# Moving the S4 kernel row's chain: vectors before denominators on GpSimd, residue product in tile 4's up place, kernel row's products and sums in three places

## The chip, the cores and the metric

One core of a Trainium2 chip (trn2) runs the kernel. Its engines are TensorE (PE in the profile), VectorE (DVE), ScalarE (ACT), GpSimd (POOL) and SyncE (SP), which here only starts transfers. The metric is the device time of one execution in microseconds.

## The reference

Input is x, 2048 rows of 512 values (2 x 1024 x 512), float32. With xn the layer norm of each row:

```
s   = causal convolution of xn, along its 512 columns, with a kernel row K, + D * xn
g   = silu( W2' ( silu(W1' xn) * (W3' xn) ) )      W' = W + 2 * B A   (LoRA, rank 16)
out = x + s * g
```

W1' and W3' are 1376 x 512, W2' is 512 x 1376. K (512 values) comes from an S4 model of 64 complex states:

```
B = Vc @ Bp ;  denom[l, n] = g[l] - Lambda[n]
k00, k01, k10, k11 = sum_n v[n] / denom[l, n]    for v = Ct*B, Ct*p, q*B, q*p (Ct, q conjugated)
K = real(ifft(c * (k00 - k01 * k10 / (1 + k11))))
```

K does not depend on x, so it is worked out once, while the first block of rows runs.

## The kernel before, in words

**Blocks and tiles.** The 2048 rows are taken as 4 blocks (`NBLK`) of 512. `body` treats one block: the 1376 hidden units are cut into 11 tiles (`HT`, j = 0 to 10) of 128, the last of 96. Each tile has three places, "gate", "up" and "down". In TensorE's program tile j is: `hidden` for W1' ("gate", into bank h1), `hidden` for W3' ("up", into h3), then `down(b, j - 1)`, the W2' product of the tile before, which adds into four banks f0 to f3. Matrices are split into a high and a low part, and `three` (lines 939 to 941) issues three matmuls per product, so `hidden` and `down` are 12 matmuls each. After tile 10 follow the last `down` and the convolution (`convolve`).

**What a tile costs the other engines.** ScalarE: silu of h1 into g (L615) and the high part of g into ghl (`hidden_hi`, L632), which waits for `g_used`, TensorE's signal that the `down` before has read ghl. VectorE: g times h3 (`hidden_mul`, L792) and the low part into ghl (`hidden_lo`, L797). Both parts of ghl are wanted by `down(b, j)`.

**Folds, first block only.** The LoRA product of each weight tile is made by TensorE in one of two spare banks (`fold`, L921 and L926), added to the raw weights by VectorE (`fold_add`, L728), rounded to the high part by ScalarE (`fold_hi`, L592), and the low part is made by VectorE (`fold_lo`, L743 or L740), three of them by GpSimd (`POOL_LO`). `folds(place, j)` says which fold stands where: (1, j+2) in gate, (3, j+2) in up, (2, j) in down. TensorE waits for the low part of (2, j) in `wait_split` ahead of `down(b, j)`, that is in tile j + 1. The two spare banks are taken in turn (`spare_table`), and a fold waits for `spare_free`, which VectorE gives after the `fold_add` of the use before. In the first block VectorE makes the low part of the last fold of a place at the start of the next place (`late`). `rows_moments` (L752, L755) for the next block also stand on VectorE at tiles 4 to 6.

**The chain of the kernel row K, first block only.** It runs beside the tiles, in this order:

1. GpSimd makes -Lambda and 2/step (`small_ready`); ScalarE scales the trigonometric rows (L671, `den_ready`, tile 1 gate).
2. GpSimd adds up the denominators and their squared magnitude (four 128x512 products and sums, `mag_ready`), then makes its three fold lows, then B and the vectors `vmat` (38 instructions on 1 to 64 columns, `v_ready`).
3. VectorE inverts mag in two halves (`RECIPROCAL_AT`, L860).
4. GpSimd multiplies by it (`res_ready`, two instructions).
5. TensorE makes the four sums over the states (L1056, `KAPPA_AT`) in a spare bank; ScalarE copies them out (L675) in its own program at the same place, and the spare bank is free only after that copy.
6. GpSimd does the complex arithmetic on 128x4 pieces, stores the coefficients (`coef_scratch`, L1268) and, when they have landed, loads them back as a row on all partitions (`coef_row`, L1273).
7. VectorE multiplies the four parts of the DFT matrix by that row (L849, `K_PRODUCTS_AT`) and sums each over its 512 columns (L853, `K_SUMS_AT`).
8. GpSimd stores the row, spreads and skews it with two more transfers into `tz`; ScalarE and GpSimd split it (tile 9 up, `tz_hi`, `tz_lo`) for the convolution.

Every engine executes its own list in order, and semaphores are all that ties the lists together. The order is written by hand, by the tables of places at the head of the file. On VectorE, within one place, the order before is: `hidden_mul` (up only), the late fold low, the fold adds, products, sums, `hidden_lo` (up only), reciprocal, moments.

Of the kernel before, what the change touches and what calls it, by code (L numbers as in the profile page):

```python
# [25 lines left out]
ALU = mybir.AluOpType  # L26
# [150 lines left out]
MOMENTS_AT_FIRST = {(4, "down"): (0,), (5, "down"): (1,), (6, "down"): (2, 3)}  # L177
MOMENTS_AT = {(r, "down"): (r,) for r in range(RT)}

RECIPROCAL_AT = [(2, "down"), (3, "down")]  # L180

KAPPA_AT = (5, "gate")
K_PRODUCTS_AT, K_SUMS_AT = (7, "gate"), (7, "up")
TOEPLITZ_AT = (9, "up")


# [60 lines left out]
def build(nc, x, xT, w1, w3, w2, lora, lora_st, lora_mv, s4_lanes, s4_vc, s4_bp, s4_scalars, trig, lanes, dft, outT):  # L247
    ctx = ExitStack()
    with ctx:
# [468 lines left out]
        def _(dve):  # L718
# [108 lines left out]
            def body(b, par, par_next, first, last):  # L827
                norm_at = NORM_AT_FIRST if first else NORM_AT
                split_at = SPLIT_AT_FIRST if first else SPLIT_AT
                moments_at = MOMENTS_AT_FIRST if first else MOMENTS_AT  # L830
                late = []
                for j in range(HT):
                    for place in ("gate", "up", "down"):
                        if place == "up" and not (first and j == 0):
                            hidden_mul(b, j)
                        if first:
                            now = folds(place, j)
                            for f_ in late:
                                fold_lo(*f_)
                            for f_ in now:  # L840
                                fold_add(*f_)
                            for f_ in now[:-1]:
                                fold_lo(*f_)
                            late = now[-1:]
                        if first and (j, place) == K_PRODUCTS_AT:
                            dve.wait_ge(dft_in, 16)
                            dve.wait_ge(coef_row_in, 16)
                            for h in range(K_PARTS):
                                nc.vector.tensor_tensor(dft_sb[:, h, :], dft_sb[:, h, :], coef_row[:, :], ALU.mult) \  # L849
                                    .then_inc(k_products, 1)  # L850
                        if first and (j, place) == K_SUMS_AT:
                            dve.wait_ge(k_products, K_PARTS)
                            nc.vector.tensor_reduce(kcol[:, :], dft_sb[:, :, :], AXIS.X, ALU.add).then_inc(k_summed, 1)  # L853
                        if place == "up":
                            hidden_lo(b, j)
                        if first and (j, place) in RECIPROCAL_AT:
                            n = RECIPROCAL_AT.index((j, place))
                            dve.wait_ge(mag_ready, 1)
                            part = mag[:, n * D // len(RECIPROCAL_AT):(n + 1) * D // len(RECIPROCAL_AT)]
                            nc.vector.reciprocal(part, part).then_inc(inv_ready, 1)  # L860
                        for c in () if last else norm_at.get((j, place), ()):
                            next_shift(b + 1, c, par_next)
                        for c in () if last else split_at.get((j, place), ()):
                            next_lo(b + 1, c, par_next)
                        for r in () if last else moments_at.get((j, place), ()):
                            rows_moments(b + 1, r)
                if not last:
                    for c in norm_at["out"]:
                        next_shift(b + 1, c, par_next)
                    for c in split_at["out"]:  # L870
                        next_lo(b + 1, c, par_next)
                if last:
                    last_sum(b, par)
                else:
                    out_sum(b, par)
# [249 lines left out]
        def _(pool):  # L1125
            steps = [0]

            def then(ins):

                steps[0] += 1  # L1130
                ins.then_inc(s4_step, 1)
                pool.wait_ge(s4_step, steps[0])
# [4 lines left out]
            def tt(out, a, c, op):  # L1137
                return nc.gpsimd.tensor_tensor(out, a, c, op)  # L1138
# [50 lines left out]


            pool.sem_inc(small_ready, 1)
            pool.wait_ge(den_ready, 3)
            then(tt(den_im[:, :], den_im[:, :], res[:, :], ALU.add))
            then(tt(mag[:, :], den_re[:, :], den_re[:, :], ALU.mult))
            then(tt(res[:, :], den_im[:, :], den_im[:, :], ALU.mult))
            tt(mag[:, :], mag[:, :], res[:, :], ALU.add).then_inc(mag_ready, 1)
            for kind, j in POOL_LO:
                fold_lo(kind, j)

            then(ts(vtmp[:, 0:1], lane_d[:, 3:4], lane_c[:, SIGN:SIGN + 1], ALU.mult))  # L1200
            then(ts(vtmp[:, 1:2], lane_d[:, 5:6], lane_c[:, SIGN:SIGN + 1], ALU.mult))
            pool.wait_ge(bvec_in, 32)
# [17 lines left out]

            ts(vmat[:, :], vmat[:, :], lane_c[:, SIGN:SIGN + 1], ALU.mult).then_inc(v_ready, 1)
            pool.wait_ge(v_ready, 1)

            pool.wait_ge(inv_ready, len(RECIPROCAL_AT))
            tt(res[0:NS, :], den_re[0:NS, :], mag[0:NS, :], ALU.mult).then_inc(res_ready, 1)
# [51 lines left out]
            rows_rstd(1, 2)  # L1277


            pool.wait_ge(k_summed, 1)  # L1280
            tt(kcol[0:1, 0:1], kcol[0:1, 0:1], scal[0:1, 0:1], ALU.add).then_inc(k_done, 1)
            pool.wait_ge(k_done, 1)
            pool.dma_start(k_row[0, P:P + D].rearrange("(p h) -> p h", h=K_PARTS), kcol[:, :]).then_inc(k_stored, 16)
# [71 lines left out]
```

## Time and profile before

| | us |
|---|---|
| median of 3 runs | 411.18 (411.14 to 411.35) |
| the profiled execution | 411.04 |
| its span (first to last instruction) | 409.2 |
| TensorE busy | 403.8 |
| VectorE, ScalarE, GpSimd busy | 169.0, 106.6, 70.7 |
| TensorE's granted clock | 1.0 of full speed in all slices |

Times of rows are counted from the start of the span. Between span and device time lie 1.84 us. A matmul's shown length overlaps the next one's; the distance between starts is what it costs. The first block takes about the first 117 us of the span.

### The profile page before, as it was taken

The page shows a single profiled execution, that of the slowest core. Times are in us where ns is not written, and L with a number is a line of the kernel's source. Part 1 is how long each engine was busy: PE and PEld are TensorE (multiplying, and loading weights), DVE is VectorE, ACT ScalarE, POOL GpSimd, SP SyncE. Part 2 cuts the span into 40 slices and gives each one's busy share as a digit, 9 for nine tenths or more (in the row PEclk, how much of TensorE's full clock was granted, in tenths as well). Part 3 has the DMA queues.
Part 4 walks back from the last instruction along what each step waited for, and adds up shares of the span by engine and source line. Part 5 has one row for each costly group of instructions (what it writes and reads, how often), then busy time and mean ns, then how long its engine had stood idle before and what let it go on. Part 6 is the DMA issues. An engine that isn't in the chain of part 4 may idle for free.

```text
span 409.2 us, 5001 instructions
## 1 busy us (share of the span) xinstructions
PE 403.8 (99%) x1850; PEld 336.9 (82%) x1850; DVE 169.0 (41%) x264; ACT 106.6 (26%) x174; POOL 70.7 (17%) x140
## 2 busy tenths in 40 slices
PE   8999999999999999999999999999999999999996
PEld 8988888878888888888888888888888888888885
DVE  5777776783792322142343222133334111211125
ACT  7654332222351111222221111112222111111122
POOL 6237737510800114000000102300000000000000
PEclk9999999999999999999999999999999999999999
DMA  7673933403425101000016101000002000000002
GB/s 267 175 274 114 318 110 89 98 9 96 154 77 181 51 2 52 2 0 0 0 48 202 61 0 52 0 0 0 0 0 103 2 0 0 2 0 0 2 0 103
DMA packets 14514, 27.02 MB, mean 66 GB/s; under 512 B 2672, under 2 KB 4720, under 8 KB 14368
## 3 DMA queue, kind: packets, MB, share of 16 engines
q1 hardware_dynamic: 13872, 25.40, 19.3%
q0 software_dynamic: 336, 0.86, 1.1%
q10 hardware_dynamic: 288, 0.52, 0.3%
q8 instruction: 11, 0.18, 0.2%
q14 instruction: 7, 0.06, 0.0%
HBM read 21.48 MB, written 4.54 MB: 64 GB/s over the span
## 4 chain that ended last, share of the span: by engine, by line
PE 93%; DVE 4%; issue 1%; ACT 0%; DVEq 0%; POOL 0%; ACTq 0%; POOLq 0%
PE h L939 19%; PE h L940 19%; PE h L941 19%; PE f L939 10%; PE f L940 10%; PE f L941 10%; PE h L962 2%; PE spare L926 2%; PE h L970 1%; DVE raw L728 1%; PE spare L941 1%; PE spare L940 1%; PE spare L939 1%; PE spare L921 1%; DVE dft_sb L849 1%
## 5 line engine op out<-in xcount | busy, mean ns | idle before, releaser
L939 PE MATMUL h<-xt,w 128*128 (+2 forms) x340 | 131.2, 386 | 0.0
L940 PE MATMUL h<-xt,w 128*128 (+2 forms) x340 | 131.1, 386 | 0.0
L941 PE MATMUL h<-xt,w 128*128 (+2 forms) x340 | 131.1, 386 | 0.0
L941 PEld LDWEIGHTS h<-xt,w 128*128 128x128 f32 x340 | 63.9, 188 | 12.9
L939 PEld LDWEIGHTS h<-xt,w 128*128 128x128 f32 x340 | 63.9, 188 | 12.7
L940 PEld LDWEIGHTS h<-xt,w 128*128 128x128 f32 x340 | 63.9, 188 | 12.5
L792 DVE TENSOR_TENSOR g<-g,h 128x512 f32<-128x512 f32 x40 | 27.5, 688 | 108.5 <-PE h L941 108.3
L939 PE MATMUL f<-ghl,w2f 128*128 128x512 f32 x176 | 68.7, 390 | 0.8 <-DVE w2f L743 0.8
L797 DVE TENSOR_TENSOR ghl<-g,ghl 128x512 fp32r<-128x512 f32 x44 | 31.6, 718 | 90.2 <-ACT ghl L632 90.2
L940 PE MATMUL f<-ghl,w2f 128*128 128x512 f32 x176 | 68.6, 390 | 0.0
L941 PE MATMUL f<-ghl,w2f 128*128 128x512 f32 x176 | 68.5, 389 | 0.0
L632 ACT CAST ghl<-g 128x512 fp32r<-128x512 f32 x44 | 27.3, 621 | 156.4 <-PE f L941 143.5
L939 PEld LDWEIGHTS f<-ghl,w2f 128*128 128x128 f32 x176 | 33.0, 188 | 7.7 <-DVE w2f L743 1.0
L941 PEld LDWEIGHTS f<-ghl,w2f 128*128 128x128 f32 x176 | 33.0, 188 | 6.9
L940 PEld LDWEIGHTS f<-ghl,w2f 128*128 128x128 f32 x176 | 33.1, 188 | 6.5
L615 ACT ACTIVATE g<-h 128x512 f32<-128x512 f32 x40 | 23.9, 598 | 45.3 <-PE h L941 45.1
L728 DVE SCALAR_TENSOR_TENSOR raw<-spare,raw 128x512 f32<-128x512 f32 (+2 forms) x33 | 22.3, 677 | 2.2 <-DVE raw L728 1.1
L1138 POOL TENSOR_TENSOR scales<-moments,lane_c 128x2 f32<-128x2 f32 x6 | 1.6, 258 | 119.5 <-DVE moments L755 119.5
L592 ACT CAST w<-raw 128x512 fp32r<-128x512 f32 (+1 forms) x22 | 13.4, 610 | 29.8 <-DVE raw L728 29.7
L1138 POOL TENSOR_TENSOR normal_rows<-xres,scale_rows 128x512 f32 (+1 forms) x12 | 16.0, 1365 | 13.5 <-DMA scale_rows<-scales_scratch 13.5
L743 DVE TENSOR_TENSOR w<-raw,w 128x512 fp32r<-128x512 f32 (+1 forms) x17 | 12.7, 751 | 0.4 <-DVE raw L728 0.2
L592 ACT CAST w2f<-raw 128x512 fp32r<-128x512 f32 (+1 forms) x11 | 6.8, 622 | 18.1 <-DVE raw L728 18.1
(133 smaller groups left out, 309.9 us busy)
## 6 DMA issues: line engine op xcount, KB each, us to landing
raw<-w_dram SPq DMA_DIRECT2D x28, 256.0 KB, 4.1
xres<-xT_dram SPq DMA_DIRECT2D x4, 1024.0 KB, 7.0
outT_dram<-xres SPq DMA_DIRECT2D x15, 256.0 KB, 2.4
rows_next<-x_dram SPq DMA_DIRECT2D x4, 512.0 KB, 3.8
scale_rows<-scales_scratch SPq DMA_DIRECT2D x3, 512.0 KB, 4.0
dft_sb<-dft_dram SPq DMA_DIRECT2D x1, 1024.0 KB, 9.3
rows<-x_dram SPq DMA_DIRECT2D x2, 512.0 KB, 6.8
raw<-w_dram SPq DMA_DIRECT2D x4, 224.0 KB, 2.5
```

What stands on the lines that cost most here:

```text
L592: nc.scalar.copy(folded(kind, j, 0), raw_tile(kind, j)).then_inc(whi_done, 1)
L615: nc.scalar.activation(g[:, :], h1[:, :], ACT.Silu).then_inc(silu_done, 1)
L632: nc.scalar.copy(ghl[:, 0, :], g[:, :]).then_inc(ghi_done, 1)
L728: nc.vector.scalar_tensor_tensor(out=rt, in0=low, scalar=LORA_SCALE, in1=rt, op0=ALU.mult, op1=ALU.add) \
L743: nc.vector.tensor_tensor(folded(kind, j, 1), raw_tile(kind, j), folded(kind, j, 0).bitcast(F32), ALU.subtract).then_inc(wlo_done, 1)
L792: nc.vector.tensor_tensor(g[:, :], g[:, :], h3[:, :], ALU.mult).then_inc(g_done, 1)
L797: nc.vector.tensor_tensor(ghl[:, 1, :], g[:, :], ghl[:, 0, :].bitcast(F32), ALU.subtract).then_inc(glo_done, 1)
L926: mm = pe.matmul(bankt[:, n * units:(n + 1) * units], fac[:, a + c * P:a + (c + 1) * P], fac[:, bc + t0 * P:bc + t0 * P + units], start=Tr ...
L939: pe.matmul(out, w[1], m[0], start=start, stop=False)
L940: pe.matmul(out, w[0], m[1], start=False, stop=False)
L941: return pe.matmul(out, w[0], m[0], start=False, stop=stop)
L1138: return nc.gpsimd.tensor_tensor(out, a, c, op)
```

## The change

Four things move; the arithmetic is the same.

- GpSimd makes B and the vectors (step 2's 38 instructions) right after `small_ready`, ahead of the denominators and the three fold lows.
- The second half of the reciprocal moves from tile 3 down to tile 3 up, and within a place the reciprocal now stands ahead of `hidden_lo`.
- The residue sums (`KAPPA_AT`) move from tile 5 gate to tile 4 up, on TensorE, on ScalarE and in the table of spare banks.
- The products with the coefficient row move from tile 7 gate (four) to tile 6 up (two) and tile 7 gate (two); the sum, one instruction over 2048 elements in tile 7 up, becomes two over 1024, in tile 7 gate and tile 7 up. Within a place the sum stands ahead of the products. GpSimd waits for both sums.

```diff
-RECIPROCAL_AT = [(2, "down"), (3, "down")]
-
-KAPPA_AT = (5, "gate")
-K_PRODUCTS_AT, K_SUMS_AT = (7, "gate"), (7, "up")
+RECIPROCAL_AT = [(2, "down"), (3, "up")]
+
+KAPPA_AT = (4, "up")
+K_PRODUCTS_AT = {(6, "up"): (0, 1), (7, "gate"): (2, 3)}
+K_SUMS_AT = {(7, "gate"): slice(0, 2), (7, "up"): slice(2, 4)}
...
-                        if first and (j, place) == K_PRODUCTS_AT:
+                        if first and (j, place) in K_SUMS_AT:
+                            parts = K_SUMS_AT[j, place]
+                            dve.wait_ge(k_products, parts.stop)
+                            nc.vector.tensor_reduce(kcol[:, parts], dft_sb[:, parts, :], AXIS.X, ALU.add).then_inc(k_summed, 1)
+                        if first and (j, place) in K_PRODUCTS_AT:
                             dve.wait_ge(dft_in, 16)
                             dve.wait_ge(coef_row_in, 16)
-                            for h in range(K_PARTS):
+                            for h in K_PRODUCTS_AT[j, place]:
                                 nc.vector.tensor_tensor(dft_sb[:, h, :], dft_sb[:, h, :], coef_row[:, :], ALU.mult) \
                                     .then_inc(k_products, 1)
-                        if first and (j, place) == K_SUMS_AT:
-                            dve.wait_ge(k_products, K_PARTS)
-                            nc.vector.tensor_reduce(kcol[:, :], dft_sb[:, :, :], AXIS.X, ALU.add).then_inc(k_summed, 1)
-                        if place == "up":
-                            hidden_lo(b, j)
                         if first and (j, place) in RECIPROCAL_AT:
...
                             nc.vector.reciprocal(part, part).then_inc(inv_ready, 1)
+                        if place == "up":
+                            hidden_lo(b, j)
...
             pool.sem_inc(small_ready, 1)
-            pool.wait_ge(den_ready, 3)
-            then(tt(den_im[:, :], den_im[:, :], res[:, :], ALU.add))
-            then(tt(mag[:, :], den_re[:, :], den_re[:, :], ALU.mult))
-            then(tt(res[:, :], den_im[:, :], den_im[:, :], ALU.mult))
-            tt(mag[:, :], mag[:, :], res[:, :], ALU.add).then_inc(mag_ready, 1)
-            for kind, j in POOL_LO:
-                fold_lo(kind, j)
-
             then(ts(vtmp[:, 0:1], lane_d[:, 3:4], lane_c[:, SIGN:SIGN + 1], ALU.mult))
...
             pool.wait_ge(v_ready, 1)
 
+            pool.wait_ge(den_ready, 3)
+            then(tt(den_im[:, :], den_im[:, :], res[:, :], ALU.add))
+            then(tt(mag[:, :], den_re[:, :], den_re[:, :], ALU.mult))
+            then(tt(res[:, :], den_im[:, :], den_im[:, :], ALU.mult))
+            tt(mag[:, :], mag[:, :], res[:, :], ALU.add).then_inc(mag_ready, 1)
+            for kind, j in POOL_LO:
+                fold_lo(kind, j)
+
             pool.wait_ge(inv_ready, len(RECIPROCAL_AT))
...
-            pool.wait_ge(k_summed, 1)
+            pool.wait_ge(k_summed, len(K_SUMS_AT))
```

What the tables do to the lists shows in two places. The first is VectorE from tile 6 up to tile 7 gate. Before (`raw` and `w` with `raw_in4` are the fold (3, 8), `raw_in1` at 448 columns is the fold (1, 9), `w2f` is the low part of (2, 6)):

```order
L728 SCALAR_TENSOR_TENSOR raw<-spare,raw 128x512 [waits fold_ready,raw_in4]
L797 TENSOR_TENSOR ghl<-g,ghl 128x512 [waits fold_added,ghi_done]
L743 TENSOR_TENSOR w_49<-raw,w_49 128x512 [waits whi_done]
L728 SCALAR_TENSOR_TENSOR raw<-spare,raw 128x512 [waits fold_ready,raw_in2]
...
L743 TENSOR_TENSOR w2f<-raw,w2f 128x512 [waits whi_done]
L728 SCALAR_TENSOR_TENSOR raw<-spare,raw 128x448 [waits fold_ready,raw_in1]
L849 TENSOR_TENSOR dft_sb<-dft_sb,coef_row 128x512 [waits fold_added,coef_row_in,dft_in]
L849 TENSOR_TENSOR dft_sb<-dft_sb,coef_row 128x512 x3
L792 TENSOR_TENSOR g<-g,h 128x512 [waits h3_ready,silu_done]
```

And now, in the same stretch (lines are one or two higher in the changed file, five for the products):

```order
L729 SCALAR_TENSOR_TENSOR raw<-spare,raw 128x512 [waits fold_ready,raw_in4]
L854 TENSOR_TENSOR dft_sb<-dft_sb,coef_row 128x512 [waits fold_added,coef_row_in,dft_in]
L854 TENSOR_TENSOR dft_sb<-dft_sb,coef_row 128x512
L798 TENSOR_TENSOR ghl<-g,ghl 128x512 [waits ghi_done]
L744 TENSOR_TENSOR w_49<-raw,w_49 128x512 [waits whi_done]
...
L744 TENSOR_TENSOR w2f<-raw,w2f 128x512 [waits whi_done]
L729 SCALAR_TENSOR_TENSOR raw<-spare,raw 128x448 [waits fold_ready,raw_in1]
L849 TENSOR_REDUCE kcol<-dft_sb 128x2 [waits fold_added,k_products]
L854 TENSOR_TENSOR dft_sb<-dft_sb,coef_row 128x512 [waits coef_row_in,dft_in]
L854 TENSOR_TENSOR dft_sb<-dft_sb,coef_row 128x512
L793 TENSOR_TENSOR g<-g,h 128x512 [waits h3_ready,silu_done]
```

The wait for the coefficient row now stands ahead of tile 6's `ghl` low part and of everything behind it, where before it stood nine instructions later, behind the low part of (2, 6).

The second place is ScalarE from tile 4 up to tile 5 gate, where the residue sums are copied out. Before:

```order
L632 CAST ghl<-g 128x512 [waits g_used,g_done]
L592 CAST w2f<-raw 128x512 [waits fold_added]
L615 ACTIVATE g<-h 128x512 [waits glo_done,h1_ready]
L592 CAST w_49<-raw 128x512 [waits fold_added]
L675 COPY kap<-spare 128x32 [waits kappa_ready]
```

And now:

```order
L633 CAST ghl<-g 128x512 [waits g_used,g_done]
L676 COPY kap<-spare 128x32 [waits kappa_ready]
L593 CAST w2f<-raw 128x512 [waits kappa_copied,fold_added]
L616 ACTIVATE g<-h 128x512 [waits glo_done,h1_ready]
L593 CAST w_49<-raw 128x512 [waits fold_added] x2
```

The copy has moved up by three instructions, to right behind tile 4's `ghl` high part, which waits for `g_used` of `down(b, 3)`; on TensorE the residue sums stand ahead of that `down`.

## Rows read from the trace of the kernel before

**Rows 1.** Waits of TensorE: us in total, times, longest us.

```profile
PE f L939 <- DVE w2f L743: 0.8, 1, 0.8
```

**Rows 2.** Timeline of TensorE, `down(b, 7)`: start us, us, line [idle before].

```profile
88.78 0.45 PE L926 MATMUL spare<-lora_stack 128*128 128x224 f32 x2
90.07 0.50 PE L939 MATMUL f<-ghl,w2f 128*128 128x512 f32 x1 [0.84 <-DVE w2f L743]
```

**Rows 3.** Timeline of VectorE, tile 6 up to tile 7 down.

```profile
74.89 0.69 DVE L797 TENSOR_TENSOR ghl<-g,ghl 128x512 fp32r<-128x512 f32 x1 [1.72 <-ACT ghl L632]
...
78.80 0.66 DVE L743 TENSOR_TENSOR w2f<-raw,w2f 128x512 fp32r<-128x512 f32 x1
...
80.22 2.50 DVE L849 TENSOR_TENSOR dft_sb<-dft_sb,coef_row 128x512 f32<-128x512 f32 x4 [0.23 <-DMA coef_row<-coef_scratch]
...
84.55 2.29 DVE L853 TENSOR_REDUCE kcol<-dft_sb 128x4 f32<-128x2048 f32 x1 [0.16 <-DVE raw L728]
...
89.32 0.69 DVE L743 TENSOR_TENSOR w2f<-raw,w2f 128x512 fp32r<-128x512 f32 x1 [0.69 <-ACT w2f L592]
```

**Rows 4.** Timeline of TensorE, tile 4 up, tile 5 gate, `down(b, 6)`.

```profile
52.48 0.40 PE L939 MATMUL f<-ghl,w2f 128*128 128x512 f32 x1
...
55.22 0.40 PE L921 MATMUL spare<-lora_stack 128*128 128x512 f32 x1
...
58.41 0.95 PE L1056 MATMUL spare<-vmat,res 128*128 128x8 f32 x8
59.22 0.47 PE L939 MATMUL h<-xt,w 128*128 128x512 f32 x1
...
79.90 0.38 PE L926 MATMUL spare<-lora_stack 128*128 128x224 f32 x2
80.12 0.41 PE L939 MATMUL f<-ghl,w2f 128*128 128x512 f32 x1
```

**Rows 5.** Timeline of ScalarE, tiles 4 and 5.

```profile
55.65 0.62 ACT L632 CAST ghl<-g 128x512 fp32r<-128x512 f32 x1
...
60.57 0.62 ACT L592 CAST w<-raw 128x512 fp32r<-128x512 f32 x1 [1.23 <-DVE raw L728]
61.10 0.18 ACT L675 COPY kap<-spare 128x32 f32<-128x32 f32 x1
```

**Rows 6.** Timeline of GpSimd, the chain from the residue sums to the coefficient row.

```profile
71.78 0.97 POOL L1268 DMA_DIRECT2D coef_scratch<-coef  x1 [0.31 <-POOL coef L1138]
...
76.21 0.58 POOL L1273 DMA_DIRECT2D coef_row<-coef_scratch  x1 [2.40 <-DMA coef_scratch<-coef]
```

**Rows 7.** Transfers: KB each, us from issue to landing.

```profile
coef_scratch<-coef POOLq DMA_DIRECT2D x1, 2.0 KB, 4.1
k_row<-kcol POOLq DMA_DIRECT2D x1, 2.0 KB, 1.7
```

**Rows 8.** SyncE's issues of weight loads, 66 to 74 us.

```profile
67.28 2.69 SPq L508 DMA_DIRECT2D raw<-w_dram  x2
72.60 0.33 SPq L508 DMA_DIRECT2D raw<-w_dram  x1
```

**Rows 9.** Timeline of GpSimd, vectors and residue products, with one VectorE row.

```profile
27.35 1.30 POOL L1138 TENSOR_TENSOR den_im<-den_im,res 128x512 f32<-128x512 f32 x1 [13.17 <-ACT res L671]
...
40.38 0.69 POOL L1135 TENSOR_SCALAR vtmp<-lane_d,lane_c 128x1 f32<-128x1 f32 x2
...
52.64 1.29 POOL L1138 TENSOR_TENSOR res<-den_re,mag 64x512 f32<-64x512 f32 x1
54.02 1.62 POOL L1138 TENSOR_TENSOR res<-den_im,mag 64x512 f32<-64x512 f32 x1
...
53.12 1.37 DVE L743 TENSOR_TENSOR w<-raw,w 128x512 fp32r<-128x512 f32 x1
```

**Rows 10.** Timeline of VectorE, tile 3 up and down.

```profile
47.20 0.71 DVE L797 TENSOR_TENSOR ghl<-g,ghl 128x512 fp32r<-128x512 f32 x1 [1.73 <-ACT ghl L632]
...
49.25 1.75 DVE L860 RECIPROCAL mag<-mag 128x256 f32<-128x256 f32 x1
```

## The prediction

> **What bounds the kernel now.** I read the busy times first: TensorE is busy 403.8 of 409.2 us, at full granted clock in every slice. So nothing that other engines do costs time unless TensorE waits for it. The view of waits, for TensorE, shows after its start-up one wait worth the name: 0.8 us for the low part of a W2' tile from VectorE [rows 1]. TensorE's own timeline places it: behind the fold pair at 88.78 the next matmul starts at 90.07 [rows 2]. The same pair is followed after 0.22 us one tile before (79.90 to 80.12) [rows 4], so `down(b, 7)` could have started at 89.00: the whole loss is **1.07 us**, and 0.1 more since the first matmul after it is slow. That is all that this change can give.
>
> The chain of waits leads back from there through VectorE. Its timeline from tile 6's `hidden_lo` at 74.89 to the low part of (2, 7) at 89.32 has no idle time but 0.23 us for the coefficient row and 0.69 for ScalarE's high part [rows 3]: a list of **14.43 us**, with the four products (2.50) and the sum (2.29) in it. TensorE starts 0.75 us after the list's last start (89.32 to 90.07). Ahead of the list VectorE is idle for 1.72 us, from 73.17 to 74.89.
>
> **The change, part by part.** I call T the time at which VectorE starts the first product.
>
> *Vectors first on GpSimd: nothing.* GpSimd is idle for 13.17 us before the denominators at 27.35, from 14.18 on; the vectors take 12.26 (40.38 to 52.64) [rows 9]. They end at 26.4, 0.9 before the denominators could start. If they ran longer, the denominators and the three fold lows would be late by what exceeds 0.9.
>
> *Reciprocal in tile 3 up: nothing.* It takes 1.75 us and finds a gap of 1.73 in front of `hidden_lo` at 47.20 [rows 10], which starts some 0.1 late; `down(b, 3)` wants it at 52.48 [rows 4]. The inverse is whole at about 47.3.
>
> *Residue products.* They now wait only for the inverse and take 3.0 us (52.64 to 55.64) [rows 9]: done at 50.4. While the first ran before, a VectorE fold low beside it took 1.37 us instead of 0.69, so each may hold one VectorE instruction for 0.7. That is paid in tile 3 down and tile 4, out of the 1.7 us that the reciprocal no longer takes there [rows 9, 10]. The fold add of (1, 6), which frees the residue sums' bank, then ends near 52.4, about when TensorE reaches them; I allow 0.1 us.
>
> *Residue sums one place earlier: 0 on TensorE, but only 4.2 us of gain for the chain.* They cost TensorE 0.81 us (58.41 to 59.22) at either place. The slot moves from 58.41 to 52.5, by 5.9 us. But ScalarE's copy stands behind tile 4's high part of ghl, and that waits for the end of `down(b, 3)`, which now comes 0.81 later since the sums stand in front of it. The high part started at 55.65, 0.43 after `down` had issued its last (55.22), so it starts at 56.3 to 56.5, and the copy, back to back, 0.53 later (60.57 to 61.10) [rows 4, 5]: 56.9 against 61.10.
>
> *GpSimd's arithmetic and the transfers: same length, other neighbours.* From the copy to the store's issue it is 10.7 us (61.10 to 71.78), to the load's issue 4.4 more, and 4.0 from there to the product at 80.22 [rows 3, 6]. All of it 4.2 earlier gives **T = 76.0**. The store took 4.1 us for 2 KB; another of 2 KB took 1.7 [rows 7]. The slow one had a weight load issued 0.8 us behind it (72.60); now, issued at 67.6, it falls between the two loads of the row at 67.28, whose second issue ends at 69.97 [rows 8]. So it costs between 1.7 and 4.1. I take 3.6, nearer to its own row, since its pieces are 8 bytes and not 16: **T = 75.5**, with ends at 73.6 and, with 0.3 of scatter on GpSimd, 76.3.
>
> *VectorE's list: +0.25.* Two products come ahead of `hidden_lo`; the list begins at T, not at 74.89. Its length: 14.43 less the wait of 0.23, plus what the sum costs more in two. A sum starts 0.16 behind the fold add that it waits for [rows 3]; now two do so: +0.16. Between 512 columns at 0.69 and 2048 at 2.29 a half lies at 1.22; two make 2.44, at most 0.15 more than one, and I take 0.09 since the start of the next overlaps the end of each a little. Sum **14.45**.
>
> *Who waits behind the new wait.* VectorE is free at 73.17 and now stands until 75.5 with tile 6's `hidden_lo`, the fold (2, 6) and all that follows behind it. The low part of (2, 6) started 3.91 after `hidden_lo` (74.89 to 78.80), so now at T + 1.21 + 3.91, and ends 0.66 later: T + 5.78 = 81.3. TensorE wants it at 80.12 [rows 4]: **a new wait of 1.2 us in tile 7's `down(b, 6)`**. Then `down(b, 7)` is ready, by TensorE's own work, at 89.00 + 1.2 = 90.2, and by VectorE at T + 14.45 + 0.75 = **90.7**: a wait of 0.5 in place of 1.07. What counts is 90.7 against 90.07: **+0.63 us**. The two cases are equal at T = 74.87, and the floor, no wait at all, is reached at T = 73.8.
> Behind `down(b, 7)` all lists stand to each other as before, only later. The kernel row's last sum ends about 1 us later; the rest of its chain moves with it and keeps its distance to tile 9 up.
>
> The profiled execution took 411.04, so the sum is 411.67. The median of the runs is 0.14 above it; the forecast for the median is **411.8**.
>
> **The rivals.**
>
> *The store is slow by itself (slower).* T stays at 76.0 or a little more. What speaks for it: the 4.1 is the only row of this very store. Against: 1.7 for the other one, and the gap between loads. Then `down(b, 7)` starts at 91.2 to 91.5: +1.1 to +1.4, or 412.3 to 412.6. It decides from T = 75.7 on.
> The Trainium skill ("DMA: Bandwidth & Descriptors", Specifications) says that pieces below 512 bytes are written by read-modify-write; by it the 8-byte store would stay slow wherever it is put, which is this rival. The 1.7 us of the 16-byte store do not bear the rule out as the whole cause.
>
> *The row is there in time (faster).* If the store takes what `k_row` took and the arithmetic runs a little shorter, T is 73.6 to 73.8, both waits go, and the gain is 1.07 to 1.17: 410.1. For it: GpSimd's small products vary, and the gap of 1.72 us on VectorE is where the products were put. Against: it needs 2.2 us less than the chain's own rows give.
>
> *The copy or the sums come late (slower).* If the bank, the inverse or the vectors are late by x, TensorE stands x ahead of `down(b, 3)` and T moves by x as well; 0.5 us makes T = 76.0. The margins above are 0.9 (vectors), 2.1 (residue products) and 0 (bank).
>
> *The change does nothing where it counts.* With T near 74.9 the old wait is only split in two, 411.2. This is part of the forecast's case.
>
> **How the numbers follow.** A difference of 0.2% is 0.82 us, about what a measurement of this kernel can tell from none. T from 74.05 to 75.7 is "same", 0.47, and holds the forecast. T above 75.7, by a slow store (0.33) or late sums (0.05): slower, 0.38. T below 74.05: faster, 0.15; the replay of the list can be off by a few tenths too, and a chain that runs beside ten others can gain in ways the rows don't show. The range goes from 410.4, which leaves out the full gain (0.15), to 412.8, above the store at 4.1 us with all scatter (0.05 left out).
>
> **What would show it.** ScalarE's copy near 56.9; the first product near 75.5, with VectorE idle before it for over 2 us on the coefficient row; TensorE waiting in `down(b, 6)` for the low part of (2, 6), about 1.2 us, and some 0.5 in `down(b, 7)`. I am wrong if the first product starts before 74, if the copy is not bound by `down(b, 3)`, or if TensorE waits anywhere ahead of tile 7.

## The result and the profile after

| | kernel before | changed kernel |
|---|---|---|
| median of 6 runs | 411.22 us (410.78 to 411.99) | 414.31 us (413.57 to 414.93) |
| the profiled execution | 411.04 us | 414.14 us |
| its span | 409.2 us | 412.3 us |
| its mean granted clock | 1.0 | 0.995 |

The ratio of the medians is **1.0075, with a 95% interval of 1.0064 to 1.0086**: slower by 3.1 us. The forecast was 0.6 us slower, and its range ended at 412.8.

The page of the changed kernel, busy times:

```profile
PE 404.4 (98%) x1850; PEld 337.5 (82%) x1850; DVE 168.7 (41%) x265; ACT 106.5 (26%) x174; POOL 71.7 (17%) x140
```

TensorE has 1850 matmuls as before and is busy 0.6 us longer over the whole span, which grew by 3.1. The total hides what happened: in the first 50 us it is busy 0.6 us less than before. Between the fold pair ahead of tile 7's `up` and the first matmul of `down(b, 7)` it was busy for 12.08 of 12.92 us before (77.15 to 90.07) and is now for 13.68 of 16.37 us (76.99 to 93.36), with 58 matmuls in both. That is 1.60 us more of work and 1.85 us more of idle time, so about half of the loss there is matmuls that ran slower. The view of waits, for TensorE from 50 to 95 us (us in total, times, longest us), names the idle time. It stands against [rows 1]:

```profile
PE h L941 <- DVE w L744: 2.7, 1, 2.7
```

The 0.8 us in a `down` are gone, and 2.7 us in an `up` are there instead. TensorE's timeline shows which one, and what follows:

```profile
76.77 0.38 PE L928 MATMUL spare<-lora_stack 128*128 128x224 f32 x2
79.84 0.47 PE L941 MATMUL h<-xt,w 128*128 128x512 f32 x1 [2.69 <-DVE w L744]
...
80.64 0.63 PE L941 MATMUL h<-xt,w 128*128 128x512 f32 x1
...
84.02 0.39 PE L943 MATMUL h<-xt,w 128*128 128x512 f32 x1
...
93.14 0.38 PE L928 MATMUL spare<-lora_stack 128*128 128x224 f32 x2
93.36 0.41 PE L941 MATMUL f<-ghl,w2f 128*128 128x512 f32 x1
```

The wait stands in front of tile 7's `up`. From 80.64 on a matmul takes 0.63 us instead of 0.39, and the next starts 0.43 behind it instead of 0.23; at 84.02 that is over. The first matmul of `down(b, 7)` comes at 93.36, against 90.07 in [rows 2]. From there to the end of the span it is 318.94 us, before 319.13. So **the whole loss lies ahead of `down(b, 7)`**.

VectorE's timeline, which answers to [rows 3]:

```profile
77.24 1.29 DVE L854 TENSOR_TENSOR dft_sb<-dft_sb,coef_row 128x512 f32<-128x512 f32 x2 [4.24 <-DMA coef_row<-coef_scratch]
78.45 0.69 DVE L798 TENSOR_TENSOR ghl<-g,ghl 128x512 fp32r<-128x512 f32 x1
79.05 0.68 DVE L744 TENSOR_TENSOR w<-raw,w 128x512 fp32r<-128x512 f32 x1
...
83.70 1.22 DVE L849 TENSOR_REDUCE kcol<-dft_sb 128x2 f32<-128x1024 f32 x1 [0.15 <-DVE raw L729]
...
91.66 0.69 DVE L744 TENSOR_TENSOR w2f<-raw,w2f 128x512 fp32r<-128x512 f32 x1 [0.69 <-ACT w2f L593]
```

The first product starts at T = 77.24, where 75.5 was forecast. VectorE stands 4.24 us on the coefficient row. The low part that TensorE waits for is at 79.05, two places behind the product. It ends at 79.73, and TensorE starts 0.11 later: **`up(b, 7)` starts at T + 2.60**. The list is 14.42 us long (77.24 to 91.66; forecast 14.45).

TensorE and ScalarE around the residue sums, which answer to [rows 4, 5]:

```profile
52.31 0.96 PE L1058 MATMUL spare<-vmat,res 128*128 128x8 f32 x8
53.12 0.48 PE L941 MATMUL f<-ghl,w2f 128*128 128x512 f32 x1
```

```profile
56.20 0.62 ACT L633 CAST ghl<-g 128x512 fp32r<-128x512 f32 x1 [1.31 <-PE f L943]
56.73 0.18 ACT L676 COPY kap<-spare 128x32 f32<-128x32 f32 x1
```

So the front of the chain came as forecast: the sums cost 0.81 at the new place, the high part of ghl waits for `down(b, 3)`, and the copy follows 0.53 behind it, at 56.73 (forecast 56.9). What comes behind did not. GpSimd's timeline, against [rows 6]:

```profile
57.05 1.17 POOL L1140 TENSOR_TENSOR cplx<-kap 128x4 f32<-128x4 f32 x2 [6.45 <-ACT kap L676]
...
65.89 1.24 POOL L1140 TENSOR_TENSOR cplx<-kap,cplx 128x4 f32<-128x4 f32 x2
...
68.41 0.97 POOL L1270 DMA_DIRECT2D coef_scratch<-coef  x1 [0.31 <-POOL coef L1140]
73.32 0.57 POOL L1275 DMA_DIRECT2D coef_row<-coef_scratch  x1 [2.88 <-DMA coef_scratch<-coef]
```

The same pairs in the kernel before, at the same places of the arithmetic:

```profile
61.42 0.49 POOL L1138 TENSOR_TENSOR cplx<-kap 128x4 f32<-128x4 f32 x2 [5.78 <-ACT kap L675]
...
70.03 0.47 POOL L1138 TENSOR_TENSOR cplx<-kap,cplx 128x4 f32<-128x4 f32 x2
```

From the copy to the store's issue it is 11.68 us, before 10.68. The two pairs shown take 1.45 us more, and the other rows about 0.4 us less. From the store's issue to the load's it is 4.91, forecast 3.93.

The windows of TensorE's wait and of the stretch behind it (its length in us, busy time of PE, PEld, DVE, ACT, POOL with counts, the granted clock, DMA share, GB/s):

```profile
76.90:79.80 2.90, 0.24 (x3) 0.06 (x1) 2.56 (x5) 0.00 (x0) 0.00 (x0) 1.00 0.00 0
79.80:83.80 4.00, 3.96 (x11) 3.15 (x12) 3.39 (x8) 1.33 (x3) 1.21 (x2) 0.59 0.20 57
```

After an idle stretch of 2.69 us the granted clock is 0.59 over 4 us, close to the lower of TensorE's two levels (1.2 GHz). TensorE is busy all the time there and gets through 11 matmuls; at the full clock it does 17 (the run of the changed kernel again, below, has that row).

### The profile page after: what moved, and what is told of

Read it like the earlier page. It is cut to its first block, busy times and chain, and to the rows that moved or that the text cites. A ratio compares the mean times of both kernels' runs of the same rounds, so it can differ in the third digit from the quotient of the medians.

```text
span 412.3 us, 5004 instructions
## 1 busy us (share of the span) xinstructions
PE 404.4 (98%) x1850; PEld 337.5 (82%) x1850; DVE 168.7 (41%) x265; ACT 106.5 (26%) x174; POOL 71.7 (17%) x140
## 4 chain that ended last, share of the span: by engine, by line
PE 90%; DVE 3%; POOL 3%; issue 2%; DMA 2%; ACT 0%; DVEq 0%; POOLq 0%; ACTq 0%
PE h L941 19%; PE h L942 19%; PE h L943 19%; PE f L941 9%; PE f L942 9%; PE f L943 9%; POOL cplx L1140 2%; PE h L964 2%; PE spare L928 1%; DMA coef_row<-coef_scratch 1%; DMA xn<-x_dram 1%; PE spare L943 1%; PE spare L942 1%; PE spare L941 1%; DVE stats L753 0%
```

## The experiments

The theory after the result, in numbers of the profiled executions: VectorE's list ties `down(b, 7)` to T + 15.17 (14.42 and 0.75), `up(b, 7)` to T + 2.60, and the span is what `down(b, 7)` starts at plus about 319.1. T came 1.74 late, and the lower clock added 0.95. The rivals were: that the earlier sums or the vectors cost something on their own; that the clock is the main thing; that the wait in `up` costs in full.

**All four products back at tile 7 gate, the sum in one at tile 7 up.** The other parts of the change stay.

```diff
-K_PRODUCTS_AT = {(6, "up"): (0, 1), (7, "gate"): (2, 3)}
-K_SUMS_AT = {(7, "gate"): slice(0, 2), (7, "up"): slice(2, 4)}
+K_PRODUCTS_AT = {(7, "gate"): (0, 1, 2, 3)}
+K_SUMS_AT = {(7, "up"): slice(0, 4)}
```

> The changed kernel with the four products back in tile 7 gate and one sum in tile 7 up; vectors first, the reciprocal in tile 3 up and the residue sums in tile 4 up stay. Theory A (all the loss comes from VectorE standing in front of the coefficient row in tile 6 up, with the low part of (3, 8) queued behind): the row is there long before tile 7 gate, no wait of TensorE in tile 7 up, the wait in down(b, 7) falls from 1.07 to about 0.84 us, time 411.0. Theory B (the residue sums one place earlier or GpSimd's new order cost time themselves): stays above 412.

Measured: 411.33 us against 411.68, ratio 0.999 (0.998 to 0.9999). VectorE's first product and TensorE's `down(b, 7)`:

```profile
80.19 2.50 DVE L854 TENSOR_TENSOR dft_sb<-dft_sb,coef_row 128x512 f32<-128x512 f32 x4 [0.23 <-DVE raw L729]
```

```profile
90.03 0.50 PE L941 MATMUL f<-ghl,w2f 128*128 128x512 f32 x1 [0.83 <-DVE w2f L744]
```

The times of the kernel before are back, within 0.04 us. So vectors, reciprocal, residue products and the earlier sums cost TensorE nothing, and **the whole loss is that of the products' and sums' place** (with their split in two, which went back with it; two runs below keep the split). A second thing is to be seen: the coefficient row is there some 3 us early (issued at 72.94, 4.4 us to landing), and the product still starts 0.23 behind the instruction before it. In [rows 3] the same 0.23 carries the name of the row's transfer, so the row cost nothing there. But it had no slack: it was issued at 76.21 and took 3.8 us, and landed at 80.0, just as VectorE came free.

**The row earlier: 16-byte pieces in the store.** The table `dft` is laid out so that the coefficients can be stored as they lie.

```diff
-...transpose(3, 4, 0, 2, 1)...
+...transpose(3, 4, 2, 0, 1)...
-pool.dma_start(coef_dram[:].rearrange("(e p c) -> p e c", e=2, c=2), coef[:, :].rearrange("p (e c) -> p e c", e=2)) \
+pool.dma_start(coef_dram[:].rearrange("(p k) -> p k", k=4), coef[:, :]) \
```

> The changed kernel, with the coefficients stored as one piece of 16 bytes per partition in place of two of 8 (the columns of the DFT matrix are ordered to match). Theory A1 (the store is slow since its pieces are 8 bytes scattered in two runs): it lands in about 1.7 us as the kernel row's store does, not 4.9; the first product starts at 74.0 instead of 77.2, TensorE's wait in tile 7 up goes, a wait of 0.3 stays in down(b, 7): 410.4. Theory A2 (the store is slow by what else moves or by queueing): lands in over 3.5, first product after 76, TensorE waits over 1 us in tile 7 up, time over 412.5.

Measured: 412.08 us against 411.68, ratio 1.001 (1.000 to 1.002); the profiled execution took 411.52. The store in the table of transfers (KB, us to landing), first of the changed kernel, then of this one:

```profile
coef_scratch<-coef POOLq DMA_DIRECT2D x1, 2.0 KB, 4.6
```

```profile
coef_scratch<-coef POOLq DMA_DIRECT2D x1, 2.0 KB, 1.9
```

Its first product, and its waits of TensorE:

```profile
75.41 1.29 DVE L854 TENSOR_TENSOR dft_sb<-dft_sb,coef_row 128x512 f32<-128x512 f32 x2 [2.27 <-DMA coef_row<-coef_scratch]
```

```profile
PE h L941 <- DVE w L744: 0.7, 1, 0.7
PE f L941 <- DVE w2f L744: 0.2, 1, 0.2
```

The store landed 2.7 us sooner, as Theory A1 has it, but T came at 75.41 and not at 74.0, and the time is 1.7 us above its 410.4: from the load's issue to the product it is 4.64 us (70.77 to 75.41) instead of 3.92. In the three runs with the 16-byte store the load took 4.3 to 4.6 us from issue to landing, in the nine others that load the same row 3.6 to 4.4. Why is open.

This run happens to have the T that was forecast for the change: 75.41, forecast 75.5. `down(b, 7)` starts at 90.58 (forecast 90.67) and the profiled execution takes 411.52 (forecast 411.67). The clock stays at 1.0. So **at this T the price was worked out rightly; T was wrong**.

**A row that is filled before the arithmetic.** The load of the row moves ahead of GpSimd's arithmetic and takes other data, so the kernel leaves out the coefficients' effect on K.

```diff
+            pool.dma_start(coef_row[:, :], trig[:, 0:D].to_broadcast([P, D])).then_inc(coef_row_in, 16)
...
-            pool.dma_start(coef_row[:, :], coef_dram[:].rearrange("(a l) -> a l", a=1).to_broadcast([P, D])) \
-                .then_inc(coef_row_in, 16)
```

> The changed kernel with the coefficient row filled from a constant row ahead of GpSimd's complex arithmetic, so VectorE never waits for it; the arithmetic and the store still run. It leaves out the coefficients' effect on K. Theory A: with the row there, the order of the change gives what it can: no wait of TensorE in tile 7, 410.0 to 410.2. If the split of the products and sums or their place costs by itself: above 411.

Measured: 410.18 us against 411.68, ratio 0.9964 (0.995 to 0.9978).

```profile
73.80 1.30 DVE L854 TENSOR_TENSOR dft_sb<-dft_sb,coef_row 128x512 f32<-128x512 f32 x2 [0.23 <-DVE raw L729]
```

T is 73.80, as early as VectorE can be; no wait of TensorE is left in this stretch, and `down(b, 7)` starts at 89.39. The place itself is good, once the row is there: 1.5 us faster than the kernel before. All of the loss hangs on the row's coming late.

**TensorE kept busy while it waits.** One more product of matmuls (the twelve of tile 6's `up` again, into the same bank ahead of the real ones) stands before the wait in `up(b, 7)`.

```diff
+                    if first and j == 7:
+                        pe.wait_ge(g_done, t)
+                        hidden(b, par, 6, 3, h3)
                     if first:
                         wait_group(pe, 3, j)
```

> The changed kernel, in which TensorE repeats tile 6's twelve up matmuls (2.73 us, results overwritten) in front of the wait for the low part of (3, 8). They fill the idle time of 2.7 us. Theory C (TensorE's clock falls after it stood idle, and nine matmuls at 0.43 us instead of 0.23 cost some 1.7 us): no slow matmuls, granted clock 1.0, 412.6. Rival (the matmuls are slow since VectorE or GpSimd are in their way there): they stay slow, 414.3.

Measured: 413.77 us against 411.68, ratio 1.0047 (1.0033 to 1.0062); the profiled execution took 414.47.

```profile
80.96 0.47 PE L941 MATMUL h<-xt,w 128*128 128x512 f32 x1 [0.60 <-DVE w L744]
```

```profile
80.90:84.90 4.00, 3.93 (x17) 3.18 (x18) 3.39 (x8) 1.32 (x3) 1.19 (x2) 1.00 0.20 57
```

The wait is 0.60 instead of 2.69 us, and 17 matmuls run in 4 us at the full clock. VectorE and GpSimd are as busy in this window as in the slow one (3.39 us in both, and 1.19 against 1.21), so they are not what slowed the matmuls. The five runs had clocks of 0.998 to 1.0; of the changed kernel's first six runs, five had 0.996 or less. But T came at 78.36, 1.1 later (copy 0.46 later, and more behind it), so the time itself did not fall to the 412.6 expected: 78.36 + 15.17 = 93.53 is where `down(b, 7)` starts. The filler shows that the list, and not TensorE's idle time as such, sets the end. As a price for the clock this run is inconclusive, since T moved too.

**The changed kernel again**, unedited, beside a new set of runs of the kernel before.

> The changed kernel again, beside the others on the same chip. 414.2 to 414.5; first product at 77.2, TensorE waits 2.7 us in tile 7 up, nine slow matmuls behind it.

Measured: 414.01 us against 411.18, ratio 1.0068 (1.0052 to 1.0084). The profiled execution took 413.50, span 411.7. Its TensorE rows and the window behind the wait:

```profile
79.93 0.47 PE L941 MATMUL h<-xt,w 128*128 128x512 f32 x1 [2.27 <-DVE w L744]
...
92.50 0.50 PE L941 MATMUL f<-ghl,w2f 128*128 128x512 f32 x1 [0.21 <-DVE w2f L744]
```

```profile
79.90:83.90 4.00, 3.92 (x17) 3.20 (x18) 3.39 (x8) 1.34 (x3) 1.21 (x2) 1.00 0.20 57
```

T was 77.33, nearly the same, and T + 15.17 is 92.50 to the hundredth. The wait was 2.27 us and the clock did not fall. So this one execution has the mechanism without the clock: 2.5 us of loss instead of 3.1. Over both sets, the seven runs of this kernel with a mean clock of 0.996 or less have a mean of 414.42 us, the three at 0.999 or 1.0 have 413.45. The T of the runs without a trace isn't known, so this alone doesn't price the clock, but it agrees with what the profiled execution says by its own rows (0.95): **about 1 us is the clock's**.

**Products at the new place, kappa at the old one.** Kappa is the code's name for the residue sums. The second half of the inverse and these sums go back, so that the row is late by the full chain.

```diff
-RECIPROCAL_AT = [(2, "down"), (3, "up")]
+RECIPROCAL_AT = [(2, "down"), (3, "down")]
-KAPPA_AT = (4, "up")
+KAPPA_AT = (5, "gate")
```

> The change's products and sums in three places alone; the residue sums in tile 5 gate and the reciprocal in tile 3 down as before, GpSimd's new order kept. T is then about 80.2. Theory A: TensorE waits 5.6 us in tile 7 up; VectorE's list gives down(b, 7) at 95.4, TensorE's way with a clock fall of 1.7 us gives 96.4: 417.5. Without a clock fall 416.6. Theory B (the other parts cost): 414 or less, as those are undone.

Measured: 417.09 us against 411.18, ratio 1.015 (1.0135 to 1.0164).

```profile
81.86 0.77 PE L941 MATMUL h<-xt,w 128*128 128x512 f32 x1 [4.76 <-DVE w L744]
...
95.15 0.41 PE L941 MATMUL f<-ghl,w2f 128*128 128x512 f32 x1
```

```profile
81.80:85.80 4.00, 3.94 (x11) 3.22 (x12) 3.39 (x8) 1.32 (x3) 1.19 (x2) 0.62 0.22 57
```

T is 79.26: `up(b, 7)` starts exactly 2.60 behind it. `down(b, 7)` starts at 95.15, where T + 15.17 gives 94.43: the clock's share is 0.72. All four runs had a clock of 0.996 or less. The earlier kappa is worth 2.0 us of T (79.26 to 77.24), not the 4.2 by which the copy moved: here the store's issue and the load's are 3.83 apart, 1.08 less than in the changed kernel, and GpSimd's arithmetic is short again:

```profile
61.20 0.49 POOL L1140 TENSOR_TENSOR cplx<-kap 128x4 f32<-128x4 f32 x2 [7.48 <-ACT kap L676]
...
71.55 0.97 POOL L1270 DMA_DIRECT2D coef_scratch<-coef  x1 [0.31 <-POOL coef L1140]
```

From the copy at 60.88 to the store's issue it is 10.67 us, as in the kernel before. So the longer arithmetic comes with the earlier start, through what runs beside it, and not with the new order of instructions.

**Moments moved, on the kernel before.** Tile 6 down has two pairs of moments in the list, 1.86 us from start to start (76.94 to 78.80 in the kernel before). Two pairs now stand in tile 4 down, two in tile 5 down and none in tile 6 down.

```diff
-MOMENTS_AT_FIRST = {(4, "down"): (0,), (5, "down"): (1,), (6, "down"): (2, 3)}
+MOMENTS_AT_FIRST = {(4, "down"): (0, 1), (5, "down"): (2, 3)}
```

> The kernel before, with nothing of the change, but the four row moments of the next block two places earlier: two in tile 4 down, two in tile 5 down, none in tile 6 down. Theory A (the limit of down(b, 7) is the length of VectorE's list from 74.89 on): the list is 1.86 us shorter, the wait of 1.07 goes, 410.0 to 410.1, the same as with the coefficient row early. Rival (VectorE's lists of tiles 4 and 5 are as tight, or the moments wait for their rows there): 411.2 or more.

Measured: 413.43 us against 411.18, ratio 1.0059 (1.0044 to 1.0074): slower, and a miss.

```profile
62.19 0.18 ACT L675 COPY kap<-spare 128x32 f32<-128x32 f32 x1
```

```profile
81.82 2.50 DVE L849 TENSOR_TENSOR dft_sb<-dft_sb,coef_row 128x512 f32<-128x512 f32 x4 [2.98 <-DMA coef_row<-coef_scratch]
```

```profile
90.33 0.48 PE L926 MATMUL spare<-lora_stack 128*128 128x224 f32 x2 [1.01 <-DVEq L732]
...
91.65 0.50 PE L939 MATMUL f<-ghl,w2f 128*128 128x512 f32 x1 [0.84 <-DVE w2f L743]
```

The added moment in tile 4 holds up the fold add behind it, ScalarE casts that tile's high part before it copies kappa, and the copy comes at 62.19 instead of 61.10 [rows 5]. The arithmetic took 11.63 us too. Its long rows stand beside VectorE's two-input instructions:

```profile
65.97 1.48 POOL L1138 TENSOR_TENSOR cplx<-cplx 128x4 f32<-128x4 f32 x3
```

```profile
66.10 0.69 DVE L797 TENSOR_TENSOR ghl<-g,ghl 128x512 fp32r<-128x512 f32 x1 [1.68 <-ACT ghl L632]
```

(A low part follows at 66.71.) The same three took 0.76 us in the kernel before. So the row came late, VectorE stood 2.98 us on it at tile 7 gate, and TensorE waited twice ahead of `down(b, 7)`. With kappa at tile 5, the kernel before has no room in tile 4.

**Both on the changed kernel: 16-byte store, moments moved.**

```diff
-...transpose(3, 4, 0, 2, 1)...
+...transpose(3, 4, 2, 0, 1)...
-pool.dma_start(coef_dram[:].rearrange("(e p c) -> p e c", e=2, c=2), ...
+pool.dma_start(coef_dram[:].rearrange("(p k) -> p k", k=4), coef[:, :]) \
-MOMENTS_AT_FIRST = {(4, "down"): (0,), (5, "down"): (1,), (6, "down"): (2, 3)}
+MOMENTS_AT_FIRST = {(4, "down"): (0, 1), (5, "down"): (2, 3)}
```

> The changed kernel with the 16-byte store and the moments moved as in the run before. Theory A, with two limits: VectorE's list ends at T + 15.17 - 1.86, TensorE's own way goes through the low part of (3, 8) at T + 2.6 and takes 11.95 from there to down(b, 7); with T = 75.4 these are 88.7 and 90.0, so the second decides: a wait of 0.9 in tile 7 up stays, 411.1, slower than the kernel before with the moments moved. Rival (only the list's length counts, as the prediction had it): 410.1.

Measured: 410.88 us against 411.18, ratio 0.9993 (0.9984 to 1.0002). T is 75.18, the only wait of TensorE is 0.52 us in `up(b, 7)`, and none is left in `down(b, 7)`. The run tells TensorE's own way from VectorE's list. The list is 13.11 us long here (75.18 to 88.29) and would allow `down(b, 7)` at 89.04, 0.75 behind its last start. TensorE's way, T + 2.60 and 11.85 us of its own matmuls from there, gives 89.63, and it started at 89.71. With kappa at tile 4 the copy stands ahead of the moved moments and is not delayed (56.85). The one wait left is that of the products' place: T is 0.6 later than `up(b, 7)` can bear, which without a wait starts at 77.15, and 77.15 − 2.60 = 74.55.

**The two products one place later, at tile 6 down.** They keep their half of the list ahead of tile 7.

```diff
-K_PRODUCTS_AT = {(6, "up"): (0, 1), (7, "gate"): (2, 3)}
+K_PRODUCTS_AT = {(6, "down"): (0, 1), (7, "gate"): (2, 3)}
```

> The changed kernel with the first two products in tile 6 down in place of tile 6 up, so the low part of ghl, the low part of (3, 8) and the fold (2, 6) stand ahead of the wait for the coefficient row. Theory A: T stays at 77.2 and the wait on VectorE at 0.3 us; TensorE doesn't wait in tile 7 up and its clock doesn't fall; it waits about 1.0 in down(b, 6) for the low part of (2, 6); down(b, 7) starts at T + 13.1 = 90.4: 411.5. Rival (the loss is the products' being split, wherever they stand): 413 or more.

Measured: 412.21 us against 411.49, ratio 1.0016 (1.0006 to 1.0025). The rows, VectorE and TensorE:

```profile
77.94 1.29 DVE L854 TENSOR_TENSOR dft_sb<-dft_sb,coef_row 128x512 f32<-128x512 f32 x2 [0.70 <-DMA coef_row<-coef_scratch]
```

```profile
81.72 0.50 PE L941 MATMUL f<-ghl,w2f 128*128 128x512 f32 x1 [0.99 <-DVE w2f L744]
```

The row is waited for 0.70 us instead of 4.24, since `hidden_lo`, the low part and a fold add stand ahead of the product now. T itself is 77.94, against 77.2 expected, and the time is 0.7 us above the 411.5 expected. The wait is in `down(b, 6)`, 1.0 us, and `down(b, 7)` starts at 91.06, 2.3 earlier than in the changed kernel. The low part that TensorE needs at 77.15 stands ahead of the wait, and with that the large loss goes. The split of products and sums is still there, so it is not what cost. What is left is a loss: any wait for the row in this stretch pushes the list.

**The place of before, with both helps.** Products at tile 7 gate, sum at tile 7 up, kappa and the rest as in the change, 16-byte store, moments moved.

```diff
-...transpose(3, 4, 0, 2, 1)...
+...transpose(3, 4, 2, 0, 1)...
-pool.dma_start(coef_dram[:].rearrange("(e p c) -> p e c", e=2, c=2), ...
+pool.dma_start(coef_dram[:].rearrange("(p k) -> p k", k=4), coef[:, :]) \
-MOMENTS_AT_FIRST = {(4, "down"): (0,), (5, "down"): (1,), (6, "down"): (2, 3)}
+MOMENTS_AT_FIRST = {(4, "down"): (0, 1), (5, "down"): (2, 3)}
-K_PRODUCTS_AT = {(6, "up"): (0, 1), (7, "gate"): (2, 3)}
-K_SUMS_AT = {(7, "gate"): slice(0, 2), (7, "up"): slice(2, 4)}
+K_PRODUCTS_AT = {(7, "gate"): (0, 1, 2, 3)}
+K_SUMS_AT = {(7, "up"): slice(0, 4)}
```

> All that the study found, together: the changed kernel's early residue sums and GpSimd order, the four products in tile 7 gate and one sum in tile 7 up as before, the 16-byte store, and the moments in tiles 4 and 5. Theory A: the row is there at 75.4, VectorE's list between 74.9 and the low part of (2, 7) is 12.3 us long, TensorE waits nowhere after its start: 410.0 to 410.2, ratio 0.997. If another limit stands close behind: 411.

Measured: 410.18 us against 411.49, ratio 0.997 (0.9958 to 0.9982). No wait of TensorE but 0.17 us before the residue sums; `down(b, 7)` at 89.28.

**The same with the old store.**

```diff
-MOMENTS_AT_FIRST = {(4, "down"): (0,), (5, "down"): (1,), (6, "down"): (2, 3)}
+MOMENTS_AT_FIRST = {(4, "down"): (0, 1), (5, "down"): (2, 3)}
-K_PRODUCTS_AT = {(6, "up"): (0, 1), (7, "gate"): (2, 3)}
-K_SUMS_AT = {(7, "gate"): slice(0, 2), (7, "up"): slice(2, 4)}
+K_PRODUCTS_AT = {(7, "gate"): (0, 1, 2, 3)}
+K_SUMS_AT = {(7, "up"): slice(0, 4)}
```

> As the run before, but with the store in pieces of 8 bytes. The row comes at 77.2 to 78.4, and the first product can't start before 78.3: at most 0.1 us worse than the run before, 410.1 to 410.3.

Measured: **410.02 us against 411.49, ratio 0.9967 (0.9955 to 0.9979)**: the fastest of all, and faster than both kernels. The store took 5.1 us and it did not matter.

```profile
78.81 2.50 DVE L854 TENSOR_TENSOR dft_sb<-dft_sb,coef_row 128x512 f32<-128x512 f32 x4 [0.22 <-DVE raw L729]
```

```profile
88.66 0.38 PE L928 MATMUL spare<-lora_stack 128*128 128x224 f32 x2
88.87 0.41 PE L941 MATMUL f<-ghl,w2f 128*128 128x512 f32 x1
```

`down(b, 7)` follows the fold pair after 0.21 us, at 88.87 where [rows 2] have 90.07: the whole of the 1.07 us, and 0.13 that lie ahead of it. The medians differ by 0.3 more (1.47), which is inside the interval. Of the moments' 1.86 us the list gives back 1.32, since VectorE now waits 0.69 us for ScalarE's high part of (2, 6). The earlier kappa did its work here in another way than by moving the products: it made room in tile 4 for the moments, and these were what the list could spare.

## Why the prediction was wrong

**Right.** The vectors first on GpSimd, the reciprocal at tile 3 up and the residue products cost nothing; the run with the products back shows it for all three at once. The copy was bound by `down(b, 3)`, at 56.73 for 56.9. The list's length was 14.42 for 14.45, with half a sum at 1.22. `down(b, 7)` starts at T + 15.17 in the three executions in which the list set it at full clock, to the hundredth. The bound on the gain, 1.07 us, is what the best run took, and 0.13 with it that lies ahead. Two readings were loose and changed little. The fold matmul at 55.22 was read as the last of `down(b, 3)`, and the high part at 55.65 as waiting for it, but its row shows no idle time in front: it stood behind another cast (at 55.12), and the copy came 0.2 earlier than forecast. And VectorE's list has further gaps of 0.15 and 0.16 us, which its length from start to start includes.

**Wrong: T.** The step "All of it 4.2 earlier gives T = 76.0", and the 0.5 us that the store was then given. It failed in two terms:

| from | forecast | measured | T by it |
|---|---|---|---|
| copy | 56.9 | 56.73 | −0.17 |
| copy to the store's issue | 10.68 | 11.68 | +1.00 |
| store's issue to load's | 3.93 | 4.91 | +0.98 |
| load's issue to the product | 4.0 | 3.92 | −0.08 |
| T | 75.5 | 77.24 | +1.74 |

Of the 0.98 us at the store, 0.5 are what I took off its own row, and 0.48 came on top (4.6 us to landing against 4.1).

For GpSimd I wrote "same length, other neighbours" and then gave the neighbours no price, though [rows 9] show one for the opposite case. In the changed kernel VectorE's timeline has a `ghl` at 56.86 and a `w` low part at 57.47, of 0.69 us each, beside the first pair of the arithmetic, and two such beside the other pair:

```profile
56.86 0.69 DVE L798 TENSOR_TENSOR ghl<-g,ghl 128x512 fp32r<-128x512 f32 x1 [2.62 <-ACT ghl L633]
57.47 0.69 DVE L744 TENSOR_TENSOR w<-raw,w 128x512 fp32r<-128x512 f32 x1
```

In the kernel before VectorE ran no instruction with two inputs in SBUF beside either pair. Each pair took about 0.7 us more. One more row met such an instruction only now and took 0.39 more; three met one before, and not now or for a shorter time, and took 0.38, 0.35 and 0.09 less. Together that is 1.02, against 1.00 measured. The Trainium skill ("GPSIMD Engine Reference", Key points) says that VectorE instructions with two inputs in SBUF contend with GpSimd; the trace agrees, 1.17 and 1.24 us against 0.49 and 0.47. The run with kappa at its old place, 10.67 us, shows that the place in time makes the length.

For the store I had named the right case as a rival and given it 0.33. My reason for the middle value was the neighbouring weight loads. That reason fell: in 8-byte pieces it took 3.5 to 5.1 us, issued anywhere from 68.41 to 73.82, and in 16-byte pieces 1.9 in all three runs. The Trainium skill's rule ("DMA: Bandwidth & Descriptors", Specifications) on pieces below 512 bytes takes in both sizes alike, so it does not explain 4.6 against 1.9. By its row [rows 7] the store had a price of 4.1, and I should have kept it.

**Wrong: where TensorE waits.** "TensorE wants it at 80.12: a new wait of 1.2 us in tile 7's `down(b, 6)`". I read only the low part of (2, 6). Ahead of it in VectorE's list stands that of W3' of tile 8, and `wait_group(pe, 3, 7)` at L1080 waits for tiles 7 and 8 together. TensorE reaches that at 77.15, and the kernel before had this low part ready:

```profile
75.50 0.69 DVE L743 TENSOR_TENSOR w<-raw,w 128x512 fp32r<-128x512 f32 x1
```

```profile
77.15 0.40 PE L939 MATMUL h<-xt,w 128*128 128x512 f32 x1
```

So TensorE bears T up to 77.15 − 2.60 = 74.55. With T at 75.5 this would not have changed the sum: TensorE needs 11.85 us from there to `down(b, 7)` (77.15 to 89.00), and 78.10 + 11.85 = 89.95 lies below the list's 90.67. The run with the 16-byte store shows just this (90.58, with 0.7 and 0.2 us of wait). At T = 77.24 the wait of 2.69 is long, and what it brought is a thing that the sum had no term for.

**Wrong: no term for the clock.** Behind the wait TensorE ran 4 us at a granted clock of 0.59. The slower matmuls cost about 1.67 us (13.52 us from `up(b, 7)` to `down(b, 7)` instead of 11.85), of which the list hides 0.72 (92.41 less 91.69), and 0.95 is left over. The miss of `down(b, 7)`, 93.36 for 90.67, is then 2.69 = 1.74 + 0.95.

The rival "the store is slow by itself" had the right sign, with its price of 1.1 to 1.4 us too small, since it left GpSimd and the clock where they were. The range had no room for both at once, the store at 4.6 and the arithmetic at +1.0.

What stays open: why the clock fell in the profiled execution of the changed kernel and not in its repeat, with a wait only 0.4 us shorter; why the load of the row took longer behind the 16-byte store; and whether it is the 8-byte piece or the two runs per partition that makes the store slow. These were not tried.

## What to carry to other kernels

A wait moved forward in an engine's list holds up everything behind it. So write down, for each instruction behind the new wait, when its reader wants it, and read the readers' wait conditions, groups included, in the code. Where a chain is moved in time, price its neighbours too: small GpSimd instructions beside VectorE's two-input ones, and a transfer by its own row. And a resource that is wanted early may be better used by leaving the consumer where it is and taking other work out of the list: here 1.3 us out of 14.4, for a gain of 1.5 us.

## What the runs showed of the hardware

- A 2 KB store to DRAM from 128 partitions took 3.5 to 5.1 us in 8-byte pieces in all ten profiled executions of that form, and 1.9 in 16-byte pieces in three; the other 16-byte store [rows 7] took 1.7.
- A pair of GpSimd instructions on 4 columns, 0.47 to 0.49 us together, took 0.7 us more when it met two VectorE instructions of 0.69 us with two inputs in SBUF. The whole arithmetic, 30 instructions, took 10.68 us before and 11.68 in the changed kernel.
- After TensorE's idle stretches of 2.69 and 4.76 us the granted clock was 0.59 and 0.62 over the 4 us that followed, and 11 matmuls ran instead of 17. After 2.27 us in the repeat, and 0.5 to 1.0 in others, the profiled executions show none of it.
- A wait that the trace puts down to a transfer can be the 0.22 to 0.23 us that stand there anyway: with the row 3 us early (0.23) or 1.4 us early (0.22) the same gap is put down to the instruction before.
